# Expert stage of a token kernel: row chunks of four and three tiles in place of three and two

## What is computed

```
posk = jnp.take_along_axis(pos, ik[:, None], axis=1)[:, 0]
keep = posk < capacity                            # capacity = int(1.2 * N / E) = 1843
xg = xpad[buf]                                    # the kept tokens of each expert
h = jnp.einsum('ecd,edh->ech', xg, W1)            # 192 -> 1024
act = h[..., :H] * jax.nn.silu(h[..., H:])        # H = 512
ye = jnp.einsum('ech,ehd->ecd', act, W2)          # 512 -> 192
out = out.at[buf.reshape(-1)].add((w_buf[..., None] * ye).reshape(E * capacity, D), mode='drop')
```

## Time and profile before

| | us |
|---|---|
| median of three runs | 4602.64 (4588.89 to 4613.26) |
| span of the profiled execution | 4494.6 |
| expert stage, first gated-layer matmul to last down matmul | 3588.6 to 4488.0 |
| PE busy, DVE, ACT, POOL over the span | 4104.2, 2885.8, 2280.9, 2368.4 |

### The profile page before, as it was taken

The page is one execution under the profiler, slowest core; times in us unless marked ns, Lnnn a source line. Parts: engine busy times, 40 slices in busy tenths (PEclk is TensorE's granted clock), DMA queues, the critical chain, the costliest instruction groups (busy, mean ns, idle before and its releaser), DMA issues. The chain is left out here.

```text
span 4494.6 us, 78782 instructions
## 1 busy us (share of the span) xinstructions
PE 4104.2 (91%) x27140; PEld 3326.2 (74%) x27140; DVE 2885.8 (64%) x8103; ACT 2280.9 (51%) x5250; POOL 2368.4 (53%) x2435
## 2 busy tenths in 40 slices
PE   3799999999999999999999999999998599999999
PEld 2576677777767676777677777767677499999999
DVE  4477777777777777677777777777775333333333
ACT  1455555556565555565555556555554233333333
POOL 2355655555555555555555555655553245555555
PEclk7799999999999999999999999999998699999999
DMA  8600000000000000000000000000000112222220
GB/s 156 105 6 11 17 10 13 9 13 9 13 11 11 11 11 14 11 11 11 16 9 14 9 13 9 13 11 11 11 9 12 49 41 50 69 75 60 74 62 20
DMA packets 159100, 122.25 MB, mean 27 GB/s; under 512 B 63839, under 2 KB 150454, under 8 KB 158710
## 3 DMA queue, kind: packets, MB, share of 16 engines
q1 hardware_dynamic: 124086, 80.29, 8.2%
q0 software_dynamic: 34624, 36.92, 3.1%
HBM read 76.84 MB, written 74.58 MB: 34 GB/s over the span
## 5 line engine op out<-in xcount | busy, mean ns | idle before, releaser
L822 ACT ACTIVATE probs<-bank_a 128x384 f32<-128x384 f32 (+2 forms) x1728 | 692.4, 453 | 648.3 <-PE bank_a L923 429.6
L1176 DVE TENSOR_REDUCE neg_max<-bank_v 128x1 f32<-128x352 f32 (+3 forms) x1728 | 778.8, 492 | 235.2 <-PE bank_v L898 127.7
L701 POOL TENSOR_SCALAR gate_tanh<-gate_tanh 128x384 f32<-128x384 f32 x320 | 386.4, 1207 | 752.0 <-ACT gate_tanh L843 750.7
L898 PE MATMUL bank_v<-heads_t 50*128 50x352 f32 (+4 forms) x1728 | 400.3, 400 | 114.0 <-DVE neg_max L1176 76.7
L898 PEld LDWEIGHTS bank_v<-heads_t 50*128 50x128 f32 (+1 forms) x1728 | 206.7, 191 | 329.6 <-DVE neg_max L1176 141.7
L941 PE MATMUL bank_o<-probs,v 128*32 128x384 f32 (+3 forms) x3456 | 444.6, 480 | 4.4 <-issue 2.3
L923 PE MATMUL bank_a<-heads_t 50*128 50x384 f32 (+3 forms) x1728 | 384.9, 386 | 30.7 <-ACT probs L822 26.3
L1483 POOL DMA_INDIRECT out_tokens<-res,token x232 | 232.5, 1002 | 331.8 <-DVE res L1669 281.8
L1060 PE MATMUL bank_a<-ffn_x,w_ffn 128*128 128x384 f32 x1600 | 383.6, 372 | 0.0
L668 POOL TENSOR_TENSOR rstd<-ve,pow_half 128x3 f32<-128x3 f32 x128 | 112.7, 881 | 476.9 <-DVE ve L1112 476.5
L1069 PE MATMUL bank_v<-w_down,hid 128*128 128x192 f32 x1920 | 354.5, 335 | 5.7 <-DVE hid L1328 4.2
(11 more groups left out here) (232 smaller groups left out, 8987.3 us busy)
## 6 DMA issues: line engine op xcount, KB each, us to landing
xs_dram<-zeros SPq DMA_DIRECT2D x29, 780.0 KB, 19.4
rows<-xs_dram SPq DMA_DIRECT2D x232, 96.0 KB
out_tokens<-h_z SPq DMA_DIRECT2D x32, 288.0 KB, 2.3
rows<-xs_dram SPq DMA_DIRECT2D x232, 33.5 KB
raw<-in_w SPq DMA_DIRECT2D x8, 512.0 KB, 4.0
raw<-in_w SPq DMA_DIRECT2D x16, 256.0 KB, 5.2
sofar<-out_tokens,token POOLq DMA_INDIRECT x232, 2.6
out_tokens<-res,token POOLq DMA_INDIRECT x232
```

The costliest lines, as they stand in the source:

```text
L701: step(pool.tensor_scalar(gate_tanh[:, m, :], gate_tanh[:, m, :], 1.0, None, ALU.add))
L822: act.activation(probs[:, n % NPROBS, i, lo:T], empty("score", k, g, kt, i)[:, lo:T], ACT.Exp, scale=DHS[k] ** -0.5).then_inc(a_free, 1)
L898: mm = pe.matmul(bank[:, 0:keys], heads_t[k][r:r + rows, b, tile[t]], heads_t[k][r:r + rows, 6 + b, 0:keys], start=True, stop=(k == 0))
L1176: dve.tensor_reduce(neg_max[k][g % 2][:, t, at:at + 1], bank[:, 0:keys], AX.X, ALU.max, negate=True).then_inc(v_free, 1)
```

## The change

The chunks of an expert are listed: `CHUNKS = (4, 4, 4, 4, 4, 3, 3, 3)`, so eight per expert and 64 in all, over the same 29 tiles. Buffers are sized for four tiles (`CT`), a chunk's first row comes from the sum of the chunks before it (`first_tile`), and every chunk now has two fills of transposed rows (the second of two tiles or of one), where a chunk of two tiles had one. The matmuls of a chunk of four are 512 columns wide.

```diff
--- before.py
+++ after.py
@@ -29,7 +29,8 @@
 E1, HF = 8, 512
 CAP = int(1.2 * N / E1)
 EROWS = -(-2 * CAP // P) * P
-NCHUNK = -(-EROWS // T)
+CHUNKS = (4, 4, 4, 4, 4, 3, 3, 3)
+CT, NCHUNK = max(CHUNKS), len(CHUNKS)
 NROWS = E1 * EROWS
 DX = D + 3
 NO_TOKEN = 16384
@@ -1362,7 +1363,11 @@
 
     def tiles(ch):
 
-        return min(NT, EROWS // P - ch % NCHUNK * NT)
+        return CHUNKS[ch % NCHUNK]
+
+    def first_tile(ch):
+
+        return sum(CHUNKS[:ch % NCHUNK])
 
     def landed(ch, n):
 
@@ -1378,17 +1383,17 @@
         raw = sb("raw", [P, 2, 2 * HF])
         w_in = [sb(f"w_in{i}", [P, 3, 2 * HF], F32R) for i in range(2)]
         w_out = [sb(f"w_out{i}", [P, NM, D]) for i in range(2)]
-        rows = sb("rows", [P, NX, NT, 2 * P + DX - D])
-
-        split_t = [sb(f"split_t{i}", [P, 4, T], F32R) for i in range(2)]
-        gated = sb("gated", [P, 2, T])
-        hid = sb("e_hid", [P, 2, NM, T])
-        res = sb("res", [P, NRES, NT, D])
-        sofar = sb("sofar", [P, NRES, NT, D])
-
-
-        token = sb("token", [P, CH, NT], I32)
-        weight = sb("weight", [P, CH, NT])
+        rows = sb("rows", [P, NX, CT, 2 * P + DX - D])
+
+        split_t = [sb(f"split_t{i}", [P, 4, CT * P], F32R) for i in range(2)]
+        gated = sb("gated", [P, 2, CT * P])
+        hid = sb("e_hid", [P, 2, NM, CT * P])
+        res = sb("res", [P, NRES, CT, D])
+        sofar = sb("sofar", [P, NRES, CT, D])
+
+
+        token = sb("token", [P, CH, CT], I32)
+        weight = sb("weight", [P, CH, CT])
         second = sb("second", [P, E1])
         first_of, second_of = sb("first_of", [P, 1]), sb("second_of", [P, 1])
         bank_a = [ctx.enter_context(nc.psum_tensor(f"e_bank_a{i}", [P, 512], F32)) for i in range(4)]
@@ -1413,7 +1418,7 @@
                     if ch:
                         a += [("y", ch - 1, t) for t in range(tiles(ch - 1))]
                     if ch + 1 < CH:
-                        v += [("x", ch + 1, 0), ("x", ch + 1, 1)][:tiles(ch + 1) - 1]
+                        v += [("x", ch + 1, 0), ("x", ch + 1, 1)]
         a += [("y", CH - 1, t) for t in range(tiles(CH - 1))]
         ea = {what: n for n, what in enumerate(a)}
         ev = {what: n for n, what in enumerate(v)}
@@ -1422,7 +1427,7 @@
 
         def last_x(ch):
 
-            return ("x", ch, tiles(ch) - 2)
+            return ("x", ch, 1)
 
         def last_y(ch):
 
@@ -1443,7 +1448,7 @@
                     if ch >= NX:
                         sp.wait_ge(ev_full, ev[last_x(ch - NX)] + 1)
                         sp.wait_ge(tagged, 2 * (ch - NX + 1))
-                    at = ch // NCHUNK * EROWS + ch % NCHUNK * T
+                    at = ch // NCHUNK * EROWS + first_tile(ch) * P
                     for t in range(tiles(ch)):
                         xs = xs_dram[at + t * P:at + (t + 1) * P, :]
                         sp.dma_start(rows[:, ch % NX, t, 0:D], xs[:, 0:D]).then_inc(rows_in[ch % NX], 16)
@@ -1523,13 +1528,13 @@
                 def transpose_rows(ch):
                     pe.wait_ge(rows_in[ch % NX], 2 * landed(ch, NX))
                     for t in range(tiles(ch)):
-                        if t != 1:
+                        if t % 2 == 0:
                             bank = fill_v("x", ch, t // 2)
                         x = rows[:, ch % NX, t]
                         at = t % 2 * 2 * P
                         pe.transpose(bank[:, at:at + P], x[:, 0:P], ident[:])
                         mm = pe.transpose(bank[:, at + P:at + 2 * P], x[:, P:2 * P], ident[:])
-                        if t:
+                        if t % 2 or t == tiles(ch) - 1:
                             mm.then_inc(ev_full, 1)
 
                 transpose_rows(0)
@@ -1579,7 +1584,7 @@
                 def rows_transposed(ch):
                     if ch >= 2:
                         act.wait_ge(ev_full, ev["a", ch - 2, NM - 1] + 1)
-                    for i in range(tiles(ch) - 1):
+                    for i in range(2):
                         what = ("x", ch, i)
                         n = min(2, tiles(ch) - 2 * i)
                         act.wait_ge(ev_full, ev[what] + 1)
@@ -1636,7 +1641,7 @@
                     x = rows[:, ch % NX]
                     dve.tensor_scalar(token[:, ch, 0:nt], x[:, 0:nt, 2 * P], float(NO_TOKEN), None, ALU.add
                                       ).then_inc(tagged, 1)
-                    tile = ch % NCHUNK * NT
+                    tile = first_tile(ch)
                     b = BOTH - tile
                     if not 0 <= b < nt:
                         dve.tensor_copy(weight[:, ch, 0:nt], x[:, 0:nt, 2 * P + 1 + (b < 0)]).then_inc(tagged, 1)
```

## The result

| | before | after |
|---|---|---|
| median of the runs, us | 4604.51 (4588.89 to 4616.36, 11 runs) | 4630.83 (4612.98 to 4641.60, 11 runs) |
| ratio | | 1.0054, 95% interval 1.0036 to 1.0073 |
| span of the profiled execution, us | 4494.6 | 4629.0, of a run of 4630.83 |

The kernel became 0.5% slower, by 26 us. The forecast was 4601 us, no change, with 4577 to 4617 as range. It was wrong.

A forecast was written before the change was run, and what follows sets the result against it. PE's own instructions were taken to bound the expert stage, with no wait left to remove. Matmuls -2.2, chunk edges 0, start +0.4 and end +0.5 gave -1.3 us from 4602.64: 4601 us, range 4577 to 4617.

The forecast's parts named there:

- the line through the two narrower widths: Gated-layer matmuls: price at 512 columns extended from 256 and 384 columns, 233.5 ns each, giving -2.2 us.
- nothing was left over per chunk: PE in the expert stage: matmuls, down matmuls and transposes fill a chunk's whole time, so fewer chunks gain 0.
- the row split had its slack: Chunk edges: ACT and DVE split the next chunk's rows during four groups; slack grows from 1.83 to about 2.3 us.
- The end: After the last down matmul: the last chunk has three tiles in place of two, +0.5 us.
- The four result banks: Chunk edges: a fourth down tile takes the second gate's bank, already read by ACT during 3.9 us of down work.
- SP's loads: Start: two more loads for the first chunk's fourth tile, landing about 0.9 us later; start priced +0.4 us, or +1.3.
- the first gather of an expert: Slower rival at an expert's start: gather waits for scatters, holding DVE's add and then PE; 4625 us, chance 0.02.
- what the sum said: Whole kernel: -2.2 matmuls, 0 chunk edges, +0.4 start, +0.5 end, together -1.3 us.
- the 0 for the chunk edges: Between chunks: 16 chunks fewer at nothing left over per chunk, so no gain or loss.
- the last rival: Slower, at an expert's first gather: landing after the last scatters, it could hold DVE and PE; 4625 us, chance 0.02.
- The slower rivals: Two cases: 512-column matmuls dearer than the line (4643 us at 260 ns, 0.06); an expert's first gather late (4625, 0.02).

The follow-up runs named there:

- e1: The kernel before, unchanged, run and profiled again in one job with the kernel after: 4609.82 us, ratio 1.0016.
- e4: The kernel after, with POOL scattering a chunk before gathering the next, so at most 8 transfers in a row: 4574.66 us, ratio 0.9915 to the kernel before.
- e9: e4 once more, side by side with e10 in five rounds: 4566.03 us, ratio 0.9906 to the kernel before.
- e7: The kernel after, with gathers as plain transfers from the row buffer in place of indirect ones from the output: 4560.81 us, ratio 0.9876 to the kernel before.
- e10: e5 once more, side by side with e9 in five rounds: 4563.81 us, ratio 0.9899 to the kernel before.
- e5: The kernel before, with POOL scattering a chunk before gathering the next, so at most 6 transfers in a row: 4577.13 us, ratio 0.9927 to the kernel before.
- e6: The kernel before, with POOL gathering two chunks ahead and a fourth result buffer, so 15 transfers in a row: 4637.26 us, ratio 1.0033 to the kernel before.
- e8: e4 with four POOL additions into an unread buffer behind each chunk's transfers: 4628.50 us, ratio 1.0051 to the kernel before.

## Why the prediction was wrong

*What held.* The distance between matmuls of 512 columns was 234 ns, on the line through the two narrower widths (233.5). The column rate plus 2.5 ns that the Trainium skill gives (page "TensorE: Matmul & The Clock Gate", section "Back-to-back issue gap") for an isolated matmul would be 215.8; this trace does not agree with it at 512 columns either. A chunk of four took 15.43 us, forecast 15.42; nothing was left over per chunk; the row split had its slack. The end, from the last down matmul on, grew from 8.1 us (e1) to 9.0, where 0.5 more was forecast. The four result banks, SP's loads and the first gather of an expert cost PE next to nothing: behind the first matmul of the stage no idle time of PE in e4, e9 and e7 is over 0.9 us. With the stalls away, the chunks are worth what the sum said, and no change is what e9 against e10 shows.

*What failed, first: the reading of the base.* The median "lies 108.0 us above that span, launch and what lies around it, which the change does not touch". What lies around a span is 1.8 us. The rest was time inside the kernel that the timed executions have and the profiled one did not. To the trace of e1 the difference is 113 us: 44 in the expert stage, by PE's stalls, 67 in the token stages, and the end. From that quick execution came "no wait of PE is left to remove".

*Second, and the step that cost the forecast its sign: "gathers and scatters keep their numbers: all go by the tile", and with it the 0 for the chunk edges.* Their number stays, 232 each; but how many POOL issues without a break does not. Where an expert ends, POOL waits until all scatters have landed, and then has two gathers, a scatter and a gather to make up: three tiles each before, 12 transfers in 15.5 us, and four each after, 16 in 20.7 us. I went through just this chain for the last rival, but asked only whether the gather lands before the add that needs it. It does. That a long row of transfers holds up an engine that waits for none of them had no row in the trace of before, where rows of 12 transfers stand without a stall, so it was not among the rivals. What the runs showed in place of the 0 is some 24 us in the stage (below). The slower rivals held 0.08 together, and half of the loss lies at the place of the last of them, at 0.02, for another reason.

*The sizes.* In the traces of e1 and after, the stage differs by 21.6 us, the medians by 26.3. The matmuls account for -2.2 of that and the rows of transfers for the rest, some 24 us. Only half of these lie at the starts of experts. Against chunks of the same place that nothing disturbs (those of the quick execution and of e7), the third and fourth chunks lose 43.5 us in e1 and 55.8 in after, 6.2 and 8.0 for each of the seven rows. The other half, 12.8 us, lies at a second place that the kernel after alone has. The step from chunks of four to chunks of three leaves POOL ten transfers without a break, and in that trace four of the eight experts have a stall in the last chunk:

```profile
3744.82 1.06 POOL L1480 DMA_INDIRECT sofar<-out_tokens,token  x1 [0.16 <-issue]
...
3756.70 0.99 POOL L1480 DMA_INDIRECT sofar<-out_tokens,token  x1 [0.30 <-issue]
...
3759.04 3.44 PE L1524 MATMUL e_bank_a<-w_out,e_hid 128*128 128x192 f32 x11 [1.80 <-issue]
```

That row lasts 12.9 us. Rows of 9 (12.1 us) stand in e1 too, and cost nothing there, so the length alone does not give the price.

*What is shown and what is not.* Shown: that the stalls go with the length of the rows, in both kernels, by shortening (e4, e5, e7) and by lengthening (e6), and that matmuls of 512 columns are not needed for them (e6) and do not bring them (e4, e9). Shown in the traces: PE's results reach ACT and DVE late while such a row lasts, and the last of them within some 2 us of its end. Loading of instructions, the rival named for e4, does not fit: ACT stands at a wait for PE's semaphore, and the stalls went when POOL's order alone was changed. Not shown: what inside the chip delays the results. Also open is why the profiled execution of before had rows of 12 without a stall or a late result, and quicker token stages; no run here gave such a one again.

## What to carry to other kernels

Compare the span of a profile with the times before anything is costed on it: if they differ by more than some us, the profiled execution is not one of those that are timed, and its idle times are not theirs. When work is cut in other pieces, count for each queue not only how many transfers it issues but how many in a row without a break. Here, waiting for an add between a chunk's transfers and the next ones was worth 28 and 45 us to the kernel before, in the two jobs of e5 and e10, where the cut into chunks by itself was worth 2.4 us of the stage.

## What the runs showed of the hardware

- While POOL issued indirect transfers without a break, PE's completions reached ACT late. From the recorded end of a tile's last down matmul to ACT's scaling of it passed up to 10.1 us in after (the fourth tile of the chunk above), 7.1 in e1, 7.9 in e6, and still 2.1 to 3.1 in the short rows of e4, e5, e9 and e10. In the quick execution of before it was 0.12 at most, in e7 0.40.
- What such a row cost PE: rows of 8 (10.2 us) next to nothing, rows of 12 (15.5 us) about 6 us per expert in e1, rows of 15 (19.7 us, e6) about 9 and rows of 16 (20.7 us, after) about 8.
- It is not the data that the transfers move: in the window of the row of 16 shown above (4030 to 4053 of the kernel after), the records of POOL's queue hold 0.01 MB in 768 packets, and the row that starts at 4277.20, with 1.57 MB, cost as much (8.3 us, where the seven rows cost 8.0 in the mean).
- A PE that was held up so came back at the lower clock: after 3.93 us without work the granted clock was 0.50, and five matmuls of 512 columns took 2.3 us in place of 1.17, so that a stall of 4 us cost more than itself.
- An fp32 add of DVE with 768 columns took 0.95 us in the mean in after and 2.82 in e8, beside additions on POOL, 4.69 at most in the lines shown.
